# Pad rows for every expert written as eight large DRAM to DRAM transfers during attention, and the last routed rows sent one tile earlier

## The reference, cut to what matters

```python
def _L0_ffn_ref(x, gate_w, gate_b, expert_bias, w1, b1, w2, b2):
    gate_logits = jnp.einsum('bsd,ed->bse', x, gate_w) + gate_b + expert_bias
    top_idx = jnp.argmax(gate_logits, axis=-1)
    out = jnp.zeros_like(x)
    for e in range(NUM_EXPERTS):                     # 8 experts, D_FF = 512
        mask = (top_idx == e)[..., None].astype(x.dtype)
        h = jax.nn.relu(jnp.einsum('bsd,df->bsf', x, w1[e]) + b1[e])
        y = jnp.einsum('bsf,fd->bsd', h, w2[e]) + b2[e]
        out = out + mask * y
    return out
x = _layernorm(x + _L0_attn_ref(x, ...))             # causal, 16 heads, clipped scores
x = _layernorm(x + _L0_ffn_ref(x, ...))
```

## Time and profile before

| | |
|---|---|
| median of 3 runs (range) | 446.91 us (446.22 to 447.86) |
| the profiled execution's own time | 446.76 us |
| its span, first to last instruction | 445.0 us |
| PE busy | 414.4 us (93%) |
| DVE busy | 361.3 us (81%) |
| ACT busy | 356.3 us (80%) |
| POOL busy | 152.8 us (34%) |
| granted TensorE clock, mean | 0.976 |
| DMA, mean over the span | 114 GB/s, 50.62 MB |

### The profile page before, as it was taken

One profiled execution on the slowest core, in us unless ns is written; L12 is line 12 of the kernel. 1 busy time (PEld: TensorE's weight loads), 2 busy tenths in 40 slices (PEclk: granted clock), 3 DMA queues, 4 the chain that ended last, 5 costly groups with the idle time before them and its releaser, 6 DMA issues. The chain is left out here.

```text
span 445.0 us, 12321 instructions
## 1 busy us (share of the span) xinstructions
PE 414.4 (93%) x4235; PEld 229.1 (51%) x4235; DVE 361.3 (81%) x824; ACT 356.3 (80%) x568; POOL 152.8 (34%) x164
## 2 busy tenths in 40 slices
PE   7899999999999999999999999998999897799970
PEld 5534344444344444434344444443345796799970
DVE  3978897999998799999888998999795586476770
ACT  3889899999988999998899999889995563466650
POOL 7221001333221112620401342240013476688882
PEclk9799999999999999999999999999999999899995
DMA  5268511478561074266202553466200456577610
GB/s 152 58 172 200 136 49 29 114 166 234 127 162 61 1 164 101 73 144 137 57 1 59 128 144 85 108 150 195 64 7 14 122 167 164 154 193 209 193 52 6
DMA packets 33005, 50.62 MB, mean 114 GB/s; under 512 B 5627, under 2 KB 16545, under 8 KB 32944
## 3 DMA queue, kind: packets, MB, share of 16 engines
q1 hardware_dynamic: 25488, 36.51, 33.7%
q10 hardware_dynamic: 5184, 9.05, 7.4%
q0 software_dynamic: 2272, 4.27, 2.9%
HBM read 21.35 MB, written 5.33 MB: 60 GB/s over the span
## 5 line engine op out<-in xcount | busy, mean ns | idle before, releaser
L1032 ACT ACTIVATE prob<-ring 128x1024 f32<-128x1024 f32 x288 | 274.5, 1040 | 25.5 <-PE ring L1224 24.6
L1242 PE MATMUL o_acc<-prob,v_stat 128*32 128x512 f32 (+3 forms) x1536 | 154.6, 497 | 2.3 <-DVE prob L705 1.4
L1224 PE MATMUL ring<-queries,keys 32*128 32x512 f32 (+3 forms) x1536 | 126.6, 384 | 0.8 <-ACT prob L1032 0.5
L1224 PEld LDWEIGHTS ring<-queries,keys 32*128 32x128 f32 x1536 | 70.5, 185 | 71.1 <-issue 45.5
L705 DVE SCALAR_TENSOR_TENSOR prob<-prob,mask_hi 128x1024 f32<-128x1024 f32 (+1 forms) x80 | 82.5, 1031 | 0.0
L691 DVE TENSOR_SCALAR prob<-prob 128x2048 f32<-128x2048 f32 x64 | 77.4, 1221 | 5.7 <-ACT prob L1032 5.3
L1120 ACT ACTIVATE prob<-ring,b1T 128x128 f32<-128x128 f32 x156 | 44.5, 368 | 37.6 <-issue 18.2
L704 DVE TENSOR_SCALAR prob<-prob 128x1024 f32<-128x1024 f32 (+1 forms) x80 | 64.4, 804 | 6.1 <-ACT prob L1032 5.4
L584 POOL DMA_INDIRECT by_expert<-xrow,index x32 | 40.8, 1276 | 78.2 <-DVE index L800 71.0
L1242 PEld LDWEIGHTS o_acc<-prob,v_stat 128*32 128x32 f32 x1536 | 33.9, 108 | 56.5 <-issue 42.1
L1365 PE MATMUL ring<-w,prob 128*128 x312 | 42.5, 280 | 6.2 <-ACT prob L1120 4.6
(11 more groups left out here) (117 smaller groups left out, 343.4 us busy)
## 6 DMA issues: line engine op xcount, KB each, us to landing
queries<-query_parts SPq DMA_DIRECT2D x60, 256.0 KB, 4.0
v_stat<-in_w ACTq DMA_DIRECT2D x34, 256.0 KB
keys<-key_parts SPq DMA_DIRECT2D x60, 128.0 KB, 2.7
queries<-by_expert SPq DMA_DIRECT2D x39, 66.0 KB
xrow<-in_x_rows SPq DMA_DIRECT2D x8, 264.0 KB, 4.4
xT<-in_x_T SPq DMA_DIRECT2D x8, 256.0 KB, 3.2
v_stat<-in_w SPq DMA_DIRECT2D x5, 256.0 KB
out<-prob,queries POOLq DMA_INDIRECT x39
```

What stands on the lines that cost most here:

```text
L1032: act.activation(prob[u % P_SLOTS][:, 2 * half:2 * half + 2, :].rearrange("p h s -> p (h s)"), slot(("score", u, half))[:], ACT.Exp, scale ...
L1224: last = pe.matmul(out[:, j % 2 * QC + off:j % 2 * QC + off + w], keys[hg][r, kt * P:(kt + 1) * P], queries[hg][r, qc, part, QC - w:QC], s ...
L1242: last = pe.matmul(o_acc[j * VW:(j + 1) * VW, QC - w:QC], v_stat[b % 2][:, hg, kt, j, :], prob[u % P_SLOTS][:, j, off:off + w], start=begi ...
```

## The change

The pads are no longer laid behind the final rows, but much earlier and much deeper. DVE copies `next_row` into `pad_at` at the head of `early_plan`, when the six halves of the first three batches have been ranked, so it holds the first free row behind them. SP then issues, before the first w1 tiles, eight transfers of 1152 rows each (1024, as many as the last batch could send to one expert, and 128) from a DRAM input straight into `by_expert`. Each is 608,256 bytes, 4.87 MB in all. The rows of the last batch are sent over them afterwards. So POOL waits, before each route of the last batch, until all eight have landed (`padded`), and SP no longer waits for pads before it loads the late tiles. The SBUF tile `pad_row` and ACT's two pad transfers are gone. The dummy rows at the end of `by_expert` come from DRAM as well. And the rows of half 7 are sent at tiles 8 and 9 instead of 9 and 10.

```diff
-ROUTE_AT = {9: (0, 1), 10: (2, 3)}
-PAD_AT = 9
-PADS_ACT = 2
+ROUTE_AT = {8: (0, 1), 9: (2, 3)}
+PAD_ROWS = S + P
...
-        def pad(eng, experts):
-            eng.wait_ge(pad_ready, 1)
-            eng.wait_ge(pad_in, 16)
-            for e in experts:
-                at = eng.value_load(pad_at[0:1, e:e + 1], min_val=0, max_val=DUMMY)
-                eng.dma_start(by_expert[bass.ds(at, P), :], pad_row[:]).then_inc(padded, 16)
...
             load_rows(0, 1)
-            sp.dma_start(pad_row[:], io["pad_rows"]).then_inc(pad_in, 16)
...
                 if b == B - 1:
                     sp.wait_ge(queries_out, len(PROJECTS))
                     sp.dma_start(b2[:], io["b2"].to_broadcast([P, E * D])).then_inc(mlp_in, 16)
+                    for q in range(Q):
+                        sp.wait_ge(routed[q], b * QT * 16)
+                    sp.wait_ge(pad_ready, 1)
+                    for e in range(E):
+                        at = sp.value_load(pad_at[0:1, e:e + 1], min_val=0, max_val=DUMMY - PAD_ROWS)
+                        sp.dma_start(by_expert[bass.ds(at, PAD_ROWS), :], io["pad_rows"]).then_inc(padded, 16)
...
                 if b == 0:
-                    sp.wait_ge(pad_in, 16)
-                    sp.dma_start(by_expert[DUMMY:DUMMY + P, :], pad_row[:]).then_inc(dummy_out, 16)
+                    sp.dma_start(by_expert[DUMMY:DUMMY + P, :], io["pad_rows"][0:P, :]).then_inc(dummy_out, 16)
...
             for c in range(EARLY_TILES):
                 load_tile(c)
-            pad(sp, range(E - PADS_ACT))
             for q in range(Q):
                 sp.wait_ge(routed[q], B * QT * 16)
-            sp.wait_ge(padded, E * 16)
             sp.wait_ge(planned, 4)
...
                 pool.wait_ge(index_ready, g + 1)
+                if g // Q == B - 1:
+                    pool.wait_ge(padded, E * 16)
                 pool.sem_inc(pool_seen, 1)
...
                 dve.wait_ge(carried, (B - 1) * Q + 1)
+                dve.tensor_copy(pad_at[:], next_row[:]).then_inc(pad_ready, 1)
...
                     dve.wait_ge(carried, B * Q + 1)
-                    dve.tensor_copy(pad_at[:], next_row[:]).then_inc(pad_ready, 1)
...
-                if PAD_AT <= c < PAD_AT + PADS_ACT:
-                    pad(act, [E - PADS_ACT + c - PAD_AT])
...
-        "pad_rows": with_ids(np.zeros((P, D), np.float32), N + np.arange(P)),
+        "pad_rows": with_ids(np.zeros((PAD_ROWS, D), np.float32), N + np.arange(PAD_ROWS)),
```

More of the change, by code:

```diff
@@ L265, in build @@
         next_row = sb("next_row", [P, E])
-        pad_row = sb("pad_row", [P, ROW])
         pad_at = sb("pad_at", [P, E], I32)
@@ L319, in build @@
         kq_in = [[sem(f"kq_in{i}{c}") for c in range(NQC)] for i in range(NHG)]
-        out_w_in, gate_in, mlp_in, pad_in = sem("out_w_in"), sem("gate_in"), sem("mlp_in"), sem("pad_in")
+        out_w_in, gate_in, mlp_in = sem("out_w_in"), sem("gate_in"), sem("mlp_in")
         ident_ready, mask_ready, upper_ready = sem("ident_ready"), sem("mask_ready"), sem("upper_ready")
```

## The result

| | kernel before | changed kernel |
|---|---|---|
| median of 20 runs (range) | 443.92 us (443.19 to 447.86) | 442.92 us (441.15 to 444.98) |
| ratio, with 95% interval | | 0.996 [0.9944, 0.9977] |
| the profiled execution's own time | 446.76 us | 443.58 us |
| its span | 445.0 us | 441.6 us |

In this comparison the changed kernel is 0.4% faster by the ratio, about 1.8 us (the medians are 1.0 us apart); 4.6 us were forecast. The median came out 0.6 us above the forecast 442.3 only because two errors met: the gain was less than half as large, and the three runs from which I subtracted (446.22 to 447.86) lie 2.3 to 3.9 us above the median of the kernel before's 20 runs, of which they are three.

What follows compares the result with a forecast made beforehand. PE's 8.9 us loss in the tail, beside the pads and last routes, was taken as the ceiling; -5.6 + 0.9 + 0.1 = -4.6 us gave a median of 442.3 us, with 8 in 10 between 439.5 and 445.3.

Steps and rivals of the forecast that it cites:

- What bounds: PE between up(11) and up(17): 20.28 us for six tiles where the pace wants 11.40; 8.9 us lost, the ceiling.
- ACT's pads: Two pad issues before relu(10) and relu(11) go: 1.8 us in all, not added to the sum.
- PE's slack: Before turn(17): without any stall PE could turn tile 17 at 376.8, 3.2 us before the forecast turn at 380.0.
- SP's pads and the routes: Six pad issues, 9.62 us, leave SP before tile 17's load; last route starts at 373.5 instead of 377.25.
- The new critical chain: Last route to tile 17's load takes 3.25 to 4.63 us; PE waits for it; up(17) gains 5.6 us (4.3 to 6.9).
- Rival A: In the tail, the stall belongs to the routes, not the pads: gain 3.7 us, 443.1 us; chance 0.16.
- The clock: PE at half clock after its new wait: 0.9 us lost, half of the earlier 1.8, ends 0 and 1.8.
- The added pads: Eight deep pads before the w1 loads: 25.0 or 16.1 us, over by 319 to 328, costing nothing.
- the rival in which they aren't done: Pads not over when the tail begins: slower, 462 us at 98 GB/s, 450.2 at 130 GB/s; chance 0.10.
- Sum: Whole kernel: -5.6 + 0.9 + 0.1 = -4.6 us, giving a median of 442.3 us.
- the CAST: One CAST added on DVE in the early plan: costs 0.1 us.

Runs made afterwards that it cites:

- pads alone: Changed kernel with half 7's routes put back to tiles 9 and 10, so only the pads are moved: 444.69 us against 445.52, ratio 0.9969.
- the repeat: Changed kernel measured once more with nothing edited, on another chip than the first comparison: 446.13 us against 445.89 for the kernel before, ratio 1.002.
- four at tile 8: Changed kernel with all four routes of half 7 behind tile 8's output write: ratio 0.9986 to the kernel before.
- one-per-tile kernel: Changed kernel with one route of half 7 behind each output write of tiles 8, 9, 10 and 11: 446.74 us, ratio 1.0011 to the kernel before.
- one, two, one: Changed kernel with half 7's routes as one behind tile 8, two behind tile 9, one behind tile 10: 442.07 us, ratio 0.9941 to the kernel before.
- short rows: Changed kernel with half 7's four routes sending 16 bytes of a row instead of 528, to their own table: 442.56 us, ratio 0.9934 to the kernel before.
- small w1 loads: Changed kernel with w1 loads of tiles 13 to 38 cut to 64 of 512 columns: 442.84 us, ratio 0.9955 to the kernel before.

## Why the prediction was right or wrong

**What bounds: right.** The loss between up(11) and up(17) was where everything could be won. Taken away whole, it gives 8.45 us of time by the medians; I had called 8.9 the ceiling.

**ACT's pads: right and nearly worthless alone.** Relu(10) waits 0.54 us instead of 1.51. I had put the gain inside PE's slack, and in the kernel with the pads alone the stall behind it is as long as ever (6.27 us).

**SP's pads and the routes: right in time.** The last route started at 373.07 (forecast 373.5), and tile 17's load 3.19 us later (forecast 3.25 to 4.63).

**The new critical chain: the step that failed.** I wrote that PE "has 3.2 us of slack, into which POOL's backlog and small stalls go, and it waits for the load". That took for granted that the stall of the results would shrink to something small once no pads ran beside it. It didn't: ACT stood 5.82 us. Up(17) came 2.98 us earlier, where the term of the sum was 5.6 with ends at 4.3 and 6.9; measured inside the stretch it is 2.5, and 1.8 in the repeat. The load was on time, and nothing waited for it. Its wait was real, but hidden under the larger one; it showed when the routes were spread.

**Rival A was the mechanism.** The stall belongs to the routes. In six traces it ends within 1.0 us of the last issue's end, though not in the kernel before (2.5 us) or with four at tile 8 (2.65 us). Its price was too good as well, 3.7, since I had moved the end of the stall with the last route and let all else follow. The stall also starts earlier then. I gave it 0.16 because half 5's four routes had made no gap of this size. That may be weak evidence, since in attention PE and ACT have units of work prepared ahead, while in the tail each tile's relu needs the up of 2 us before. No run here tests that. Nearer evidence stood in the trace of the kernel before, and I had not read it: the four routes of half 6, sent in a row at the start of the tail. POOL's last of them, then DVE's and ACT's waits beside it:

```profile
345.11 0.96 POOL L584 DMA_INDIRECT by_expert<-xrow,index  x1 [0.31 <-issue]
```

```profile
346.87 0.29 DVE L974 TENSOR_TENSOR prob<-ring,prob 128x128 f32<-128x128 f32 x1 [5.09 <-remote]
```

```profile
345.49 1.14 ACT L1120 ACTIVATE prob<-ring,b1T 128x128 f32<-128x128 f32 x4 [2.10 <-issue]
```

DVE stands "remote" there too, with no pad in flight, and goes on 0.8 us behind the last issue's end. That speaks for rival A. Against its size: DVE is only 2.1 us behind the modelled end of down(0) (344.74), ACT goes on before the last issue has ended, and PE stands 0.6 us.

**The clock: too low, and inside its ends by luck.** I took 0.9 us, half of what it had cost, with 0 and 1.8 as ends. The drop came in full: down(11) and up(13) took 1.01 and 0.60 us more than at full clock, 1.6 in all, behind a hole that was longer than I had forecast and stood elsewhere.

**The added pads: right.** 16.3 us, against bounds of 16.1 and 25.0, over by 319.6, so the rival in which they aren't done fell. My estimate of 27 us, which counted the bytes read and written, was 10.7 us too long. The w1 loads started behind the pads, as laid out. The first turn of the tail was 0.2 us later. POOL's new wait cost nothing.

**Sum.** Forecast -5.6 + 0.9 + 0.1 = -4.6. Measured -1.8 by the ratio, and nothing in the repeat; the stretch from up(9) to up(17) gives -2.5 and -1.8 with the clock drop in it. The 0.1 us for the CAST is too small for any run here to show.

What stays open: how closely issued indirect transfers keep PE's results from ACT and DVE, and where the limit lies. No run separates POOL's issuing from what the DMA engines then do: every kernel that kept the routes kept their number of rows. In the one-per-tile kernel pairs of a write and a route stood 1.34 to 1.40 us apart, at most two in a row, and nothing was held; with three in a row 1.26 to 1.34 us apart (one, two, one) ACT stood 4.8 us. Output writes 1.8 to 1.9 us apart never did this in the tail. These points are consistent with "three in a row", but half 6's four routes in a row held ACT and DVE far less, and the spacing was not varied by itself.

## What to carry to other kernels

When an engine waits for another's results though the profile has these long finished, look for what is being issued at that moment and take it out in an experiment before pricing a change: one run without the four transfers would have told 8 us from 0. A wait that a change would uncover is only worth pricing once the one above it is known to go. And where the effect is below 1%, compare stretches inside the traces as well as times, because the start of the tail wandered by 3.8 us from trace to trace here.

## What the runs showed of the hardware

- With three or more of POOL's indirect transfers in a row beside tiles 8 to 10, issued 1.26 to 1.34 us apart, ACT stood 4.0 to 6.7 us for results of PE that the profile has finished; neither 33 times fewer bytes nor 8 times smaller w1 loads beside them ended it, and without the transfers it was gone. In six traces of five kernels ACT went on 0.1 to 1.0 us after the last issue ended; in the kernel before and with four at tile 8 it took 2.5 and 2.65 us, and with short rows or small w1 loads the first part of the stall ended 0.1 us before the third issue did. Half 6's four routes, at the start of the tail, held DVE no more than 2.1 us in the kernel before.
- A DRAM to DRAM copy of 4.87 MB in rows of 528 bytes laid one behind another ran at 298 GB/s, close to the fastest stretch of the earlier trace rows (302), and disturbed attention little: between traces with the same stretches of half clock in attention, the tail began 0.2 to 0.5 us later with early pads (339.44 us against 338.92, 340.73 against 340.38 and 340.56).
- After a hole of 2.8 to 5.6 us PE ran at half clock for either 3.4 or 6.8 us, without a clear relation to the length of the hole (5.5 us: 3.4; 3.1 us: 6.8; 2.81 us: 3.4 in one kernel, 6.8 in another).
